# Attention over graph quads: the next quad's scores placed between the products of the first and second unit, one-hots two quads ahead

## The chip, the cores and the metric

The kernel runs on one NeuronCore of a Trainium2 chip. The metric is the device time of one launch in microseconds; less is better. All data starts and ends in HBM; each engine (TensorE = PE, VectorE = DVE, ScalarE = ACT, GpSimd = POOL, SyncE = SP) runs its own instruction stream and waits for the others by semaphores.

## The reference, cut to what matters

`x` is [3125, 768]; there are 50,000 edges `src -> dst`, sorted by `dst`. A two-layer GCN runs first, then one graph attention layer (12 heads of 64), which is the part that the change touches:

```
x = x + GCN(relu(layernorm(x)), edges)            # not touched
h = relu(layernorm(x))
ft = h @ W_fc.T per head;  a1 = <ft, attn_l>;  a2 = <ft, attn_r>
e = leaky_relu(a1[src] + a2[dst], 0.2)
alpha = segment softmax of e over dst             # max, exp, sum, divide
agg = segment_sum(alpha * ft[src], dst)
out = x + relu(h @ W_res.T per head + agg)
```

## The kernel before, in words

The 3125 target nodes are 25 tiles of 128, and a tile is four units of 32 nodes. The edges into a tile are handled in quads. A quad gives each unit four chunks of 128 edges of its own (16 columns of 128 edges) and one shared chunk (column QX = 16). In this data a tile has one quad, so there are 25 quads, and `nth < 1` always holds. The last tile has 53 nodes, so two units (`LU`).

For each quad, GpSimd issues 17 indirect DMAs (`fetch`, line L1089). Each gathers 128 rows of `table3` (12 heads x 65 numbers and the 12 source terms, 792 floats) into `ring`, which has room for two quads. So the gathers of quad q+2 need the room of quad q: `fetch` waits on `used[s]` before the four gathers of unit s, and on `used[US]` before that of the shared chunk. TensorE raises `used[s]` when the products of that unit are done.

What is done for a quad q:

- `next_hot` (VectorE, L1360) makes the one-hot matrix edge -> target; `turn_hot` (PE L1267, ACT L1177) transposes it; `cast_hot` (ACT L1191) makes it float32 for the products.
- `take_terms` (VectorE, L1366 and L1367) copies the source terms out of the ring. It first waits in `rows_landed` for all 17 gathers of its quad.
- `scores` (PE, L1278 to L1285) adds the target terms and the source terms in `ps_s`; only L1285 needs the terms.
- `sloped` (ACT, L1183) multiplies by 0.2; VectorE takes the maximum (L1415), two scans (L1418, L1421: the segment maximum forward and back) and subtracts (L1423).
- PE transposes (L1295), ACT takes the exponential (L1205, `weight`).
- The rows are scaled by the weights in place: units 0 to 2 and the shared chunk by VectorE (L1438 three times, L1443), unit 3 by ACT (L1216, 48 instructions).
- `unit(s)` (PE, L1313, 16 matmuls) multiplies the one-hots into the accumulators; L1324 does the shared chunk.
- The tile before is finished in between: `divide` (VectorE, L1372 to L1376), `natural` (PE, L1236 and L1242), `finish` (VectorE, L1382), then a store.

The order of each engine is written out by hand; there is no scheduler. SyncE loads the slots (indices, two quads ahead), the masks of the scans, and moves the tiles.

## Time and profile before

| | us |
|---|---|
| median of 3 runs | 2235.81 |
| lowest and highest | 2234.13, 2235.86 |
| profiled execution, own time | 2237.61 |
| its span | 2235.8 |
| POOL busy in the span | 1314.7 |
| TensorE, mean granted clock | 0.877 |

The span is the time from the first to the last instruction that the profiler saw. The attention stage is the part from about 1400 us on. A row of the timeline gives start, duration, engine, line, operation, output and inputs, count, and in brackets how long the engine was idle before it and what released it.

### The profile page before, as it was taken

What the parts mean: (1) busy time and instruction counts of PE and PEld (TensorE: products, weight loads), DVE (VectorE), ACT (ScalarE), POOL (GpSimd) and SP (SyncE); (2) the same over time, 40 slices, a digit from 0 to 9 for tenths busy, and PEclk for the clock granted to TensorE, in tenths of its full rate; (3) what the DMA queues carried; (4) which work ended last, traced back from release to release, by engine and by line L of the source; (5) the groups of instructions that cost most, each with busy time, mean ns of one, the idle gap of its engine ahead of it and who ended that gap; (6) DMA issues with size and microseconds to landing.
All of it is one profiled execution on the core that took longest, in us unless ns stands there. A gap on an engine that the chain in (4) does not pass through costs nothing. (4 is left out here: it accounts for less than half of the span.)

```text
span 2235.8 us, 50371 instructions
## 1 busy us (share of the span) xinstructions
PE 1464.5 (66%) x17861; PEld 979.8 (44%) x17862; DVE 839.6 (38%) x1256; ACT 529.1 (24%) x1690; POOL 1314.7 (59%) x1294
## 2 busy tenths in 40 slices
PE   3242787887888578888788867265556555555564
PEld 3141555555555345555555556143334334433442
DVE  9840111111111112222222234365566556655662
ACT  0300011010110000000000026244554455435543
POOL 2014777777776477777777600787665665666530
PEclk9998999999999779999999989578887787878877
DMA  5219999999998599999999826778666766677640
GB/s 186 114 69 281 342 328 331 335 328 333 334 329 296 183 337 329 329 330 326 334 334 329 293 80 271 253 263 291 239 233 224 278 241 222 241 267 256 211 169 33
DMA packets 140710, 587.00 MB, mean 263 GB/s; under 512 B 31465, under 2 KB 33217, under 8 KB 140539
## 3 DMA queue, kind: packets, MB, share of 16 engines
q0 software_dynamic: 100272, 497.49, 63.5%
q1 hardware_dynamic: 33285, 69.50, 8.6%
q10 hardware_dynamic: 7110, 19.43, 2.4%
q8 instruction: 27, 0.44, 0.1%
q14 instruction: 16, 0.13, 0.0%
HBM read 534.62 MB, written 51.71 MB: 262 GB/s over the span
## 5 line engine op out<-in xcount | busy, mean ns | idle before, releaser
L570 POOL DMA_INDIRECT ring_c<-table,slot_c x834 | 794.8, 953 | 323.3 <-issue 300.5
L1089 POOL DMA_INDIRECT ring<-table,slot x417 | 497.5, 1193 | 256.3 <-PE ps_acc L1313 134.6
L1313 PE MATMUL ps_acc<-ring,hot_f 128*32 128x195 f32 x3136 | 183.9, 385 | 183.2 <-ACT ring L1216 117.7
L1216 ACT ACTIVATE ring<-ring,weight x1200 | 290.4, 336 | 0.6
L602 ACT ACTIVATE slot_c<-units 128x8 int32 (+1 forms) x104 | 21.7, 210 | 1058.8 <-DMA ring_c<-table,slot_c 995.6
L1438 DVE TENSOR_TENSOR ring<-ring,weight 128x3120 f32 x73 | 246.3, 3401 | 0.4 <-ACT weight L1205 0.4
L699 DVE TENSOR_TENSOR hots<-iota,units 128x256 f32<-128x256 bf16 x102 | 43.6, 429 | 477.5 <-PE ps_sum0a L655 155.9
L1313 PEld LDWEIGHTS ps_acc<-ring,hot_f 128*32 128x32 f32 x3136 | 104.1, 125 | 249.4 <-ACT ring L1216 127.3
L687 PE MATMUL ps_yb<-weights,sum_tb 128*128 128x512 f32 (+1 forms) x600 | 202.4, 494 | 2.1 <-DVE nodes L730 2.1
L687 PE MATMUL ps_ya<-weights,sum_ta 128*128 128x512 f32 (+1 forms) x600 | 201.9, 493 | 2.1 <-DVE nodes L726 2.1
L655 PE MATMUL ps_sum0a<-ring_c,hots 128*32 128x192 f32 x2000 | 107.6, 374 | 80.0 <-DMA ring_c<-table,slot_c 73.4
L687 PEld LDWEIGHTS ps_yb<-weights,sum_tb 128*128 128x128 f32 x600 | 112.9, 192 | 90.2 <-issue 83.8
L687 PEld LDWEIGHTS ps_ya<-weights,sum_ta 128*128 128x128 f32 x600 | 112.6, 191 | 89.9 <-issue 83.4
L655 PE MATMUL ps_sum0b<-ring_c,hots 128*32 128x192 f32 x2000 | 107.9, 375 | 61.0 <-DMA ring_c<-table,slot_c 54.2
L655 PE MATMUL ps_sum1b<-ring_c,hots 128*32 128x192 f32 x1920 | 100.2, 368 | 48.5 <-DMA ring_c<-table,slot_c 41.1
L1415 DVE TENSOR_TENSOR score<-ps_s,top_g 48x640 f32<-48x640 f32 x25 | 20.5, 818 | 277.9 <-ACT top_g L1183 277.9
L655 PEld LDWEIGHTS ps_sum0a<-ring_c,hots 128*32 128x32 f32 x2000 | 75.4, 124 | 111.9 <-issue 75.9
L655 PE MATMUL ps_sum1a<-ring_c,hots 128*32 128x192 f32 x1920 | 93.5, 348 | 45.6 <-DMA ring_c<-table,slot_c 37.6
L1295 PE MATMUL ps_s<-ident,score 48*128 48x48 f32 x125 | 18.4, 305 | 152.1 <-DVE score L1423 152.1
L655 PEld LDWEIGHTS ps_sum0b<-ring_c,hots 128*32 128x32 f32 x2000 | 75.1, 125 | 93.1 <-issue 62.7
L655 PEld LDWEIGHTS ps_sum1b<-ring_c,hots 128*32 128x32 f32 x1920 | 72.0, 123 | 76.5 <-issue 55.0
L655 PEld LDWEIGHTS ps_sum1a<-ring_c,hots 128*32 128x32 f32 x1920 | 66.8, 116 | 71.8 <-issue 53.8
(238 smaller groups left out, 1680.9 us busy)
## 6 DMA issues: line engine op xcount, KB each, us to landing
ring_c<-table,slot_c POOLq DMA_INDIRECT x834, 5.4
table<-ft SPq DMA_DIRECT2D x25, 396.0 KB, 2.7
table<-nodes SPq DMA_DIRECT2D x25, 384.0 KB, 3.3
table<-nodes ACTq DMA_DIRECT2D x25, 384.0 KB, 5.2
turned_table<-h_t SPq DMA_DIRECT2D x25, 384.0 KB, 2.3
turned_g<-turned_table SPq DMA_DIRECT2D x25, 384.0 KB, 5.9
nodes<-in_x ACTq DMA_DIRECT2D x24, 384.0 KB
out_x<-nodes SPq DMA_DIRECT2D x24, 384.0 KB
```

The costliest lines, as they stand in the source:

```text
L570: eng.indirect_dma_start(out=ring[:, t * QH + k, :], out_offset=None, in_=table, in_offset=bass.IndirectOffsetOnAxis(ap=slot[t][:, k:k + 1 ...
L602: eng.activation(slot[t][:, :], units[:, ds(q, 1), t * QH:(t + 1) * QH + t].rearrange("p a c -> p (a c)"), ACT.Copy).then_inc(slot_ready[t ...
L655: last = eng.matmul(block_of(par, s, g), hot, rows[:, g * GB:(g + 1) * GB], start=start, stop=True, skip_group_check=True)
L687: last = eng.matmul(ps_y[:, c0:c0 + n], sum_t[:, k, :], w[:, k, c0:c0 + n], start=(k == 0), stop=(k == KB - 1))
L699: eng.tensor_tensor(hots[k][:, :, :].rearrange("p (s c) d -> p s c d", c=CPU), iota0[:, :].unsqueeze(1).unsqueeze(2).to_broadcast([P, 2, C ...
L1089: eng.indirect_dma_start(out=ring[:, b * RB + at * FROW:b * RB + (at + 1) * FROW], out_offset=None, in_=table3, in_offset=bass.IndirectOff ...
L1216: last = eng.activation(head, head, ACT.Copy, scale=weight[:, c, mine * H + h:mine * H + h + 1])
L1295: last = eng.transpose(ps_e[:, c, :], score[:, 1 + c * P:1 + (c + 1) * P], ident[0:UH, 0:UH])
L1313: last = eng.matmul(acc_of(s, g), hot_f[:, c, s * UD:(s + 1) * UD], ring[:, x0 + g * GW:x0 + (g + 1) * GW], start=False, stop=True, skip_g ...
L1415: eng.tensor_tensor(score[:, 1:1 + WIN], window(0, WIN), top[:, 1:1 + WIN], ALU.max).then_inc(z_made, 1)
L1438: eng.tensor_tensor(mine, mine, weight[:, 0:CPU, s * H:(s + 1) * H].unsqueeze(3).to_broadcast([P, CPU, H, FH]), ALU.mult).then_inc(scaled[ ...
```

## The change

The change reorders four engines inside a quad and moves two steps across quads.

- VectorE: `take_terms(q + 1)` stood at the end of quad q and now stands after the scaling of unit 0. `next_hot(q + 1)`, which stood before the scalings, becomes `next_hot(q + 2)` at the end of the quad.
- TensorE: `turn_hot(q + 1)` moves ahead of `natural`, and `scores(q + 1)` from behind all products to between unit 0 and unit 1.
- ScalarE: `sloped(q + 1)` is done in the middle of the scaling of unit 3 in quad q, not at the start of quad q+1.
- GpSimd: the gather of the shared chunk is asked for ahead of those of the last unit.

```diff
--- before.py
+++ after.py
@@ -1025,6 +1025,10 @@
             def units_of(j):
                 return LU if isinstance(j, int) and j == NT - 1 else US
 
+
+            def early_of(j):
+                return min(1, units_of(j) - 1)
+
             def node(j):
                 return nodes[:, ds(j, 1), :].rearrange("p a d -> p (a d)")
 
@@ -1089,14 +1093,11 @@
                                 eng.indirect_dma_start(out=ring[:, b * RB + at * FROW:b * RB + (at + 1) * FROW], out_offset=None, in_=table3,
                                                        in_offset=bass.IndirectOffsetOnAxis(ap=slot[:, b, at:at + 1], axis=0)).then_inc(landed[b][s], 16)
                             eng.wait_ge(slot_in, q * 16 + 16)
-                            for s in range(nu):
+                            for s in list(range(nu - 1)) + [US, nu - 1]:
                                 eng.wait_ge(used[s], q + 1)
                                 eng.sem_inc(passed, 1)
-                                for c in range(CPU):
-                                    ask(s * CPU + c, s)
-                            eng.wait_ge(used[US], q + 1)
-                            eng.sem_inc(passed, 1)
-                            ask(QX, US)
+                                for at in (QX,) if s == US else range(s * CPU, (s + 1) * CPU):
+                                    ask(at, s)
                         by_parity(eng, eng.snap(q % 2), gather)
                     last_q, total = quad_bounds(eng)
                     with eng.Fori(0, last_q) as q:
@@ -1194,7 +1195,6 @@
                         mine = units_of(j) - 1
 
                         def follow(q, nth, left):
-                            sloped(q)
                             cast_hot(q, j)
                             with eng.If(nth < 1):
                                 eng.sem_inc(r_exp, 1)
@@ -1214,10 +1214,13 @@
                                 for h in range(H):
                                     head = rows[:, c * FROW + h * FH:c * FROW + (h + 1) * FH]
                                     last = eng.activation(head, head, ACT.Copy, scale=weight[:, c, mine * H + h:mine * H + h + 1])
+                                if c == CPU - 3:
+                                    sloped(q + 1)
                             last.then_inc(scaled[mine], 1)
                         tile_quads(eng, j, follow)
                     turn_hot(0)
                     a2_of(0)
+                    sloped(0)
                     tiles(eng, step)
 
                 @block.tensor
@@ -1294,6 +1297,7 @@
                             for c in range(UC):
                                 last = eng.transpose(ps_e[:, c, :], score[:, 1 + c * P:1 + (c + 1) * P], ident[0:UH, 0:UH])
                             last.then_inc(t_made, 1)
+                            by_parity(eng, eng.snap(q % 2), lambda b: turn_hot(q + 1, 1 - b))
                             with eng.If(nth < 1):
                                 eng.sem_inc(r_hot, 1)
                                 eng.sem_inc(r_all, 1)
@@ -1304,19 +1308,22 @@
                             with eng.Else():
                                 rescale(q, j)
 
-                            def products(b):
-                                def unit(s):
-                                    eng.wait_ge(scaled[s], q + 1)
-                                    for c in range(CPU):
-                                        x0 = b * RB + (s * CPU + c) * FROW
-                                        for g in range(US):
-                                            last = eng.matmul(acc_of(s, g), hot_f[:, c, s * UD:(s + 1) * UD], ring[:, x0 + g * GW:x0 + (g + 1) * GW],
-                                                              start=False, stop=True, skip_group_check=True)
-                                    return last.then_inc(used[s], 1)
-                                turn_hot(q + 1, 1 - b)
-                                eng.wait_ge(hot_cast, q + 1)
-                                for s in range(nu - 1):
-                                    unit(s)
+                            def unit(b, s):
+                                eng.wait_ge(scaled[s], q + 1)
+                                for c in range(CPU):
+                                    x0 = b * RB + (s * CPU + c) * FROW
+                                    for g in range(US):
+                                        last = eng.matmul(acc_of(s, g), hot_f[:, c, s * UD:(s + 1) * UD], ring[:, x0 + g * GW:x0 + (g + 1) * GW],
+                                                          start=False, stop=True, skip_group_check=True)
+                                last.then_inc(used[s], 1)
+
+                            def first_products(b):
+                                for s in range(early_of(j)):
+                                    unit(b, s)
+
+                            def other_products(b):
+                                for s in range(early_of(j), nu - 1):
+                                    unit(b, s)
                                 eng.wait_ge(scaled[US], q + 1)
                                 x0 = b * RB + QX * FROW
                                 for s in range(nu):
@@ -1324,9 +1331,12 @@
                                         last = eng.matmul(acc_of(s, g), hot_f[:, CPU, s * UD:(s + 1) * UD], ring[:, x0 + g * GW:x0 + (g + 1) * GW],
                                                           start=False, stop=True, skip_group_check=True)
                                 last.then_inc(used[US], 1)
-                                unit(nu - 1)
-                            by_parity(eng, eng.snap(q % 2), products)
+                                unit(b, nu - 1)
+                            eng.wait_ge(hot_cast, q + 1)
+                            eng.sem_inc(passed, 1)
+                            by_parity(eng, eng.snap(q % 2), first_products)
                             scores(q + 1)
+                            by_parity(eng, eng.snap(q % 2), other_products)
                         tile_quads(eng, j, visit)
                     turn_hot(0, 0)
                     scores(0)
@@ -1429,7 +1439,6 @@
                                     divide(j - 1, q)
                             with eng.Else():
                                 rescale(q, nu)
-                            next_hot(q + 1)
                             eng.wait_ge(w_made, q + 1)
                             par = eng.snap(q % 2)
                             rows = ring[:, ds(eng.snap(par * RB), RB)].rearrange("p (c f) -> p c f", f=FROW)[:, :, 0:H * FH].rearrange("p c (h x) -> p c h x", x=FH)
@@ -1438,18 +1447,23 @@
                                 eng.tensor_tensor(mine, mine, weight[:, 0:CPU, s * H:(s + 1) * H].unsqueeze(3).to_broadcast([P, CPU, H, FH]), ALU.mult).then_inc(scaled[s], 1)
                                 if s == 0:
                                     eng.tensor_reduce(weight_x[:, :], weight[:, CPU, :].rearrange("p (s h) -> p h s", h=H), mybir.AxisListType.X, ALU.add).then_inc(wx_made, 1)
+                                if s == early_of(j) - 1:
+                                    take_terms(q + 1)
                             eng.wait_ge(wx_made, q + 1)
                             shared = rows[:, QX, :, :]
                             eng.tensor_tensor(shared, shared, weight_x[:, :].unsqueeze(2).to_broadcast([P, H, FH]), ALU.mult).then_inc(scaled[US], 1)
                             if has_before(j):
                                 with eng.If(nth < 1):
                                     finish(j - 1)
-                            take_terms(q + 1)
+                            eng.wait_ge(hot_cast, q + 1)
+                            next_hot(q + 2)
                         return tile_quads(eng, j, visit)
                     bounds = quad_bounds(eng)
-                    next_hot(0)
+                    for b in range(2):
+                        next_hot(b)
                     take_terms(0)
                     tiles(eng, step)
+                    eng.sem_inc(c_chain, 2)
                     divide(NT - 1, bounds[1])
                     finish(NT - 1)
 
```

In TensorE's stream for one quad (tiles 1 to 23, even quads), before; L1278 and L1285 are the scores of the next quad, L1313 the products of the units:

```order
L1295 MATMUL ps_s<-ident,score 128x48 x5
L1236 MATMUL ps_n<-wres_b,turned_g 128x128 x6
L1242 MATMUL ps_n<-o_g,ident 32x192 x16
L1267 MATMUL ps_s<-ident_b,hot 128x128 x5
L1313 MATMUL ps_acc<-ring,hot_f 32x195 x48
L1324 MATMUL ps_acc<-ring,hot_f 32x195 x16
L1313 MATMUL ps_acc<-ring,hot_f 32x195 x16
L1278 MATMUL ps_s<-hot_t,a_blk 48x128
L1285 MATMUL ps_s<-ident,terms 48x128 x5
```

And TensorE's stream at the same place in the changed kernel, where L1270 is the old L1267, L1281 the old L1278, L1316 the old L1313 and L1331 the old L1324:

```order
L1298 MATMUL ps_s<-ident,score 128x48 x5
L1270 MATMUL ps_s<-ident_b,hot 128x128 x5
L1239 MATMUL ps_n<-wres_b,turned_g 128x128 x6
L1245 MATMUL ps_n<-o_g,ident 32x192 x16
L1316 MATMUL ps_acc<-ring,hot_f 32x195 x16
L1281 MATMUL ps_s<-hot_t,a_blk 48x128
L1288 MATMUL ps_s<-ident,terms 48x128 x5
L1316 MATMUL ps_acc<-ring,hot_f 32x195 x32
L1331 MATMUL ps_acc<-ring,hot_f 32x195 x16
L1316 MATMUL ps_acc<-ring,hot_f 32x195 x16
```

The scores of the next quad (L1281 to L1288) have moved ahead of 48 + 16 of the 80 products, and the transposes of the one-hots (L1270) ahead of L1239 and L1245.

In VectorE's stream for one quad, before; L1438 are the scalings, L1366 and L1367 the terms of the next quad:

```order
L1360 TENSOR_TENSOR hot<-iota,slot 128x640
L1438 TENSOR_TENSOR ring<-ring,weight 128x4x780
L1440 TENSOR_REDUCE weight_x<-weight 128x12
L1438 TENSOR_TENSOR ring<-ring,weight 128x4x780
L1438 TENSOR_TENSOR ring<-ring,weight 128x4x780
L1443 TENSOR_TENSOR ring<-ring,weight_x 128x780
L1382 SCALAR_TENSOR_TENSOR nodes<-ps_n,nodes 128x768
L1366 COPY terms<-ring 128x4x4x12
L1367 COPY terms<-ring 128x48
```

And VectorE's stream in the changed kernel, where L1376 and L1377 are the old L1366 and L1367, L1447 the old L1438, L1454 the old L1443, L1392 the old L1382 and L1370 the old L1360:

```order
L1447 TENSOR_TENSOR ring<-ring,weight 128x4x780
L1449 TENSOR_REDUCE weight_x<-weight 128x12
L1376 COPY terms<-ring 128x4x4x12
L1377 COPY terms<-ring 128x48
L1447 TENSOR_TENSOR ring<-ring,weight 128x4x780
L1447 TENSOR_TENSOR ring<-ring,weight 128x4x780
L1454 TENSOR_TENSOR ring<-ring,weight_x 128x780
L1392 SCALAR_TENSOR_TENSOR nodes<-ps_n,nodes 128x768
L1370 TENSOR_TENSOR hot<-iota,slot 128x640
```

The terms of the next quad, with the wait for its landed rows, now stand ahead of the scalings of units 1 and 2 and of the shared chunk; the one-hots went from the front to the end.

## Rows read from the trace of the kernel before

**Rows 1.** Waits, 1700 to 2200 us: who for whom, total, times, longest.

```profile
DVE score L1415 <- ACT top_g L1183: 199.3, 16, 13.1
POOL ring L1089 <- PE ps_acc L1313: 107.1, 20, 9.5
```

**Rows 2.** Timeline of one quad.

```profile
1744.85 0.70 ACT L1183 ACTIVATE top_g<-ps_s 48x640 f32<-48x640 f32 x1 [5.74 <-PE ps_s L1285]
...
1745.58 0.82 DVE L1415 TENSOR_TENSOR score<-ps_s,top_g 48x640 f32<-48x640 f32 x1 [11.69 <-ACT top_g L1183]
...
1746.68 1.49 DVE L1418 TENSOR_TENSOR_SCAN top_g<-same_g,score 48x641 f32<-48x641 bf16 x1 [0.28 <-DVE score L1415]
...
1749.78 0.82 DVE L1423 TENSOR_TENSOR score<-score,top_g 48x640 f32<-48x640 f32 x1
...
1751.53 0.37 ACT L1205 ACTIVATE weight<-ps_s 128x240 f32<-128x240 f32 x1 [5.35 <-PE ps_s L1295]
...
1751.85 0.82 DVE L1360 TENSOR_TENSOR hot<-iota,slot 128x640 bf16 x1
...
1752.58 3.40 DVE L1438 TENSOR_TENSOR ring<-ring,weight 128x3120 f32 x1
...
1756.05 6.71 DVE L1438 TENSOR_TENSOR ring<-ring,weight 128x3120 f32 x2
...
1756.85 1.53 PE L1313 MATMUL ps_acc<-ring,hot_f 128*32 128x195 f32 x32
...
1758.45 11.62 ACT L1216 ACTIVATE ring<-ring,weight  x48
1759.24 1.03 POOL L1089 DMA_INDIRECT ring<-table,slot  x1 [5.75 <-PE ps_acc L1313]
...
1762.68 0.96 DVE L1443 TENSOR_TENSOR ring<-ring,weight_x 128x780 f32 x1
...
1763.56 0.95 DVE L1382 SCALAR_TENSOR_TENSOR nodes<-ps_n,nodes 128x768 f32 x1
...
1770.12 2.83 PE L1313 MATMUL ps_acc<-ring,hot_f 128*32 128x195 f32 x32 [4.45 <-ACT ring L1216]
...
1777.33 0.70 ACT L1183 ACTIVATE top_g<-ps_s 48x640 f32<-48x640 f32 x1 [7.26 <-PE ps_s L1285]
```

**Rows 3.** Timeline of the first quad: gathers beside scalings, the landing, and products.

```profile
1440.91 3.41 DVE L1438 TENSOR_TENSOR ring<-ring,weight 128x3120 f32 x1 [0.39 <-ACT weight L1205]
...
1442.12 3.02 POOL L1089 DMA_INDIRECT ring<-table,slot  x1 [0.30 <-issue]
...
1444.46 2.83 PE L1313 MATMUL ps_acc<-ring,hot_f 128*32 128x195 f32 x32 [2.88 <-DVE ring L1438]
1445.45 3.14 POOL L1089 DMA_INDIRECT ring<-table,slot  x1 [0.31 <-issue]
...
1452.22 0.95 POOL L1089 DMA_INDIRECT ring<-table,slot  x1 [0.30 <-issue]
...
1458.37 0.26 DVE L1366 COPY terms<-ring 128x192 f32 x1 [6.40 <-DMA ring<-table,slot]
```

**Rows 4.** Timeline: gathers that begin during a scan and a one-hot.

```profile
1747.77 1.15 POOL L1089 DMA_INDIRECT ring<-table,slot  x1 [0.30 <-issue]
...
1752.06 1.43 POOL L1089 DMA_INDIRECT ring<-table,slot  x1 [0.30 <-issue]
```

**Rows 5.** Gathers (L1089) from 1480 to 2200 us: issue to landing.

```profile
DMA to landing us min/median/max: 4.4/5.1/5.8
```

**Rows 6.** Windows: busy (instructions) of PE, PEld, DVE, ACT, POOL; PEclk, DMA, GB/s.

```profile
1442.00:1445.00 3.00, 0.54 (x8) 0.46 (x12) 3.00 (x3) 2.94 (x13) 2.88 (x1) 0.50 0.82 279
```

**Rows 7.** Timeline of the last quad.

```profile
2198.14 0.37 ACT L1205 ACTIVATE weight<-ps_s 128x240 f32<-128x240 f32 x1 [5.21 <-PE ps_s L1295]
...
2216.93 2.83 PE L1313 MATMUL ps_acc<-ring,hot_f 128*32 128x195 f32 x32 [11.07 <-ACT ring L1216]
...
2222.43 1.60 PE L1236 MATMUL ps_n<-wres_b,turned_g 128*128 128x128 f32 x12
```

## Prediction

> **What bounds the kernel now.** The page first: POOL is busy for 1314.7 of 2235.8 us (the table above) and no engine is near its span, so the question is which wait ends last. The waits of 1700 to 2200 us (16 quads) show two that matter: DVE waits 199.3 us for `sloped`, 12.5 us a quad, and POOL waits 107.1 us for products to free the ring [rows 1]. The timeline of one quad gives the ring of steps [rows 2]: `sloped` at 1744.85, maximum, two scans, subtraction at 1749.78, weights done at 1751.90, three scalings on DVE to 1762.76; beside them ACT scales unit 3 from 1758.45 to 1770.07, then unit 3's products, then the next quad's scores, and `sloped` again at 1777.33. The reader is to see that scores stand last although nothing in them needs the products. From the weights of this quad (1751.53) to those of the last (2198.14 [rows 7]) are 14 periods of 31.9 us. A quad costs that, 25 times over.
>
> **What the change does to this ring.** It takes the scores, and ACT's wait for unit 3, off the path. On DVE a quad then needs only its own work of [rows 2], so I step through it with the start of the copy of the next quad's terms as 0, durations from [rows 2]:
> - second scaling 0.3 to 3.7 (6.71 for two, so the next starts 3.3 later), third 3.6 to 7.0, shared chunk 6.9 to 7.9, `finish` to 8.8, one-hots 8.7 to 9.5, maximum at 9.4;
> - scans: the first starts 1.10 after the maximum, 10.5 to 12.0, the second to 13.6; subtraction at 13.6; weights done 2.12 after that start (1749.78 to 1751.90), 15.7; first scaling of the next quad from 15.95 to 19.35;
> - then the next copy, if its rows are there: a period of about 20 us. ACT (scalings in two halves of 5.8, `sloped` at about 3.8) has unit 3 ready at 10.3 and is not later. The same count for PE: unit 3's products start by 10.4, its loop has time until 14.7.
>
> So compute alone would go from 31.9 to 20 us. I don't forecast that, because of a wait that the change adds.
>
> **The wait that it adds.** The copy waits for all 17 gathers of quad q+1 (second order difference: it now stands ahead of the scalings of units 1 and 2). Queued behind it on DVE are the scalings of units 1 and 2 of quad q, behind these on PE the products of unit 1, and behind these on POOL the gathers into unit 1's room for quad q+2. POOL can issue only four (unit 0's) before it stands. Before, unit 1's scaling waited for no gather. Priced as a ring:
> - last gather issued to landed: 5.1 (median of 4.4 to 5.8 [rows 5]; 5.89 for the last gather that DVE waited for [rows 3]: 1452.22, copy at 1458.37), plus 0.26 from landing to copy: 5.36;
> - copy and second scaling to 3.7; unit 1's products from 3.75. They take 1.53 at full clock [rows 2] and 2.83 at half. Which? PE will have been idle some 7 us before the scores' last part, as in the first quad, where PEclk was 0.50 through a stretch with 0.54 us of products in 3 us [rows 6] and the first products took 2.83 [rows 3]. I take 2.83: 6.6;
> - products to the first gather 0.86 (1758.38 to 1759.24 [rows 2]): 7.44.
>
> Thirteen gathers are left (four each of units 1, 2, 3, and the shared one). Unhindered, one takes 0.95 and the next follows after 0.30: 12 x 1.25 = 15.0 to the start of the last. Sum without hindrance 7.44 + 15.0 + 5.36 = 27.8.
>
> **The port.** POOL's gathers are hindered by DVE. In the first quad the gathers of 1442.12 and 1445.45 took 3.02 and 3.14: each ended 0.82 after a scaling did (1444.32 + 0.82 = 1445.14) [rows 3]. One begun in a scan took 1.15, in a one-hot 1.43 [rows 4]. Gathers beside the maximum, which reads PSUM, took 0.95. Before, POOL met one or two scalings a quad and stood idle for the others; now its 13 gathers run against nearly all of DVE's work. Stepping, each hindered gather ending 0.82 (0.76 for scans) after the operation:
> 7.44 (shared scaling, ends 8.7), 9.0 (one-hots, 10.3), 10.6 (scan, 12.8), 13.1 (scan, 14.3), 14.6, 15.9, 17.1 (first scaling, 19.35 + 0.82 = 20.2), 20.5, and five more 1.25 apart: the 13th starts at 26.7. Plus 5.36: **32.1 us**. The cover is gone: hindrance costs 4.3.
>
> The Trainium skill ("SBUF — State Buffer", "SBUF: two separate sides") says more: whichever of the two starts first keeps the pair for its whole instruction, so a gather under way would hold DVE up too. By that each of about four operations here would start up to 0.8 us later and the period be some 1 to 2 us longer. The trace disagrees where it can be seen: the gather of 1759.24 lay across the start of a scaling, and the two scalings took 6.71 together [rows 2]. The sum does without it.
>
> **The ends.** Start: in quad 0 the rows of quad 1 come earlier, since DVE no longer scales beside the last gathers (3.02 to 3.14 each [rows 3]): the 15th still starts at 1445.45, the 17th at 1447.95 instead of 1452.22, the copy at 1454.1 instead of 1458.37. Then 22 periods of 32.1 to the copy in quad 22: 2160.3. The last quad has nine gathers, not 17: stepping as above, the last ends its hindrance at 20.2, so the last copy of a loaded quad comes 24.5 later: 2184.8. Weights 15.7 later: 2200.5, against 2198.51 before [rows 7]. After the weights, before: ACT's unit at 18.4, end at 37.3. Now transposing no longer waits for `natural` (about 5 us), but `sloped` in mid-scaling waits for the scores behind unit 0: ACT's unit at 16.6, and the 2.7 us of scores between unit 1's products and `natural` (2219.76 to 2222.43 [rows 7]) are gone: end at 32.9. Sum: 2200.5 + 32.9 = **2233.4** for the profiled span of 2235.8, that is 2.4 less; the profiled execution's own time is 2237.61 and the median 1.8 lower, so 2235.81 - 2.4 = 2233.
>
> Edits that I cost at nothing: one-hots two quads ahead (slots are loaded two ahead, and the wait for `cast_hot` is met since before the weights; 0.8 of DVE if not hidden); the shared chunk asked for before the last unit (POOL follows PE's order; up to one gather, 1.25, if it didn't).
>
> **Rivals.** A measurement of this kernel can tell 0.2%, so no change is 2231.3 to 2240.3.
> - *A. As summed*, 32.1 a period: 2233, own range 2222 to 2245 (landing 4.8 to 5.5, so 0.3 to 0.4 in 22 periods). 0.40.
> - *B. Unit 1's products at full clock.* The scores' last part wakes PE. One gather more fits before the scans: 1.25 less, 30.8, 2233 - 27 = 2206. For it: PE has work just before; in the first quad the second unit took 1.75. Against: the clock in [rows 6]. If it comes with C it is near 2230. 0.28.
> - *C. One gather more is caught (slower).* The first scaling starts at 15.95, and the sixth of the 13 gathers at 15.88, 0.07 earlier. If the scaling is first, that gather takes until 20.1 and all later ones shift by 1.1 to 1.25; the same if it starts late, up to 17.1, since then the seventh is held longer. It decides when the weights are 0.1 us earlier or over 0.6 later, as by unit 3's products at half clock (2.83 [rows 2]). 33.2 a period: 2233 + 24 = 2257. 0.26.
> - *D. Gathers don't bind.* Rows land before DVE wants them and the period falls toward 20 to 28: 22 x 4.3 = 95 less at 27.8, 2138. For it: 17 gathers need 21.3 us. Against: the ring of waits above holds even unhindered. 0.06.
>
> **How the numbers follow.** Faster by over 0.2%: B but its mixed part, 0.24, D 0.06, the lower part of A 0.14: 0.44. Same: A 0.18, B 0.04, C 0.02: 0.24. Slower: C 0.24, A 0.08: 0.32. The likeliest is A. The range leaves out D and the far side of C with a landing of 5.8 (22 x 0.4 more): 2200 to 2262.
>
> **What would show it.** Right: in the changed profile DVE waits about 10 us a quad before the copy of the terms for DMA, POOL waits about 5 us before the gathers of unit 1 for products, gathers of 1.3 to 4.2 us stand beside scans and scalings, and `sloped` is no longer what DVE waits for. PE's products of unit 1 at 2.83 tell A from B; how many gathers start between the second scan and the first scaling tells C. Wrong: a period under 28, rows that land before DVE has done the first scaling, or a wait for unit 3 ahead of the weights.

## The result: the change is 0.3% slower here, and the profile after

| | before | after |
|---|---|---|
| median, us (9 runs each, same chip) | 2235.86 | 2243.34 |
| lowest and highest, us | 2233.99, 2240.58 | 2238.82, 2248.07 |
| profiled execution, own time and span, us | 2237.61, 2235.8 | 2243.34, 2241.6 |
| mean granted clock of TensorE | 0.877 | 0.860 |

The ratio is 1.0032, 95% interval 1.0022 to 1.0042: slower by 0.3%, small but clear of the noise. 2233 with "faster" as the likeliest sign was forecast; the time lies in the range, on the other side of no change.

The waits of the changed kernel, 1700 to 2200 us, answer to [rows 1] (who for whom, total, times, longest):

```profile
DVE terms L1376 <- DMA ring<-table,slot: 205.8, 16, 14.0
ACT top_g L1184 <- DVEq L1421: 202.6, 16, 13.9
PE ps_s L1288 <- DVE terms L1377: 143.3, 16, 10.4
POOL ring L1093 <- PE ps_acc L1316: 97.8, 21, 7.2
```

VectorE no longer waits for `sloped`. In its place it waits 205.8 us for the rows of the next quad to land, before the copy of the terms: 12.9 us a quad, against 12.5 for `sloped` before. One wait was exchanged for another of the same size. POOL waits 6.1 us a quad (97.8 us in 16 quads) for products to free its room. Both are near the signs that the prediction named (about 10 and about 5). The page has the same over the whole span (out<-in, count, then busy and mean ns of one, then idle before):

```profile
L1093 POOL DMA_INDIRECT ring<-table,slot x417 | 504.9, 1211 | 283.0 <-PE ps_acc L1316 153.8
L1376 DVE COPY terms<-ring 128x192 f32 (+1 forms) x26 | 7.1, 272 | 331.3 <-DMA ring<-table,slot 331.3
```

Two successive quads in the timeline of the changed kernel. First one that took 33.0 us from copy to copy:

```profile
1712.03 0.43 DVE L1376 COPY terms<-ring 128x192 f32 x1 [12.83 <-DMA ring<-table,slot]
...
1715.92 2.83 PE L1316 MATMUL ps_acc<-ring,hot_f 128*32 128x195 f32 x32 [0.88 <-DVE ring L1447]
...
1719.59 1.29 POOL L1093 DMA_INDIRECT ring<-table,slot  x1 [7.22 <-PE ps_acc L1316]
...
1722.79 1.99 POOL L1093 DMA_INDIRECT ring<-table,slot  x1 [0.30 <-issue]
...
1725.63 0.82 DVE L1433 TENSOR_TENSOR score<-score,top_g 48x640 f32<-48x640 f32 x1
...
1726.60 0.48 PE L1298 MATMUL ps_s<-ident,score 48*128 48x48 f32 x5 [2.29 <-DVE score L1433]
1726.66 0.94 POOL L1093 DMA_INDIRECT ring<-table,slot  x1 [0.30 <-issue]
...
1727.11 0.37 ACT L1205 ACTIVATE weight<-ps_s 128x240 f32<-128x240 f32 x1 [1.85 <-issue]
...
1727.70 3.41 DVE L1447 TENSOR_TENSOR ring<-ring,weight 128x3120 f32 x1
...
1727.90 4.03 POOL L1093 DMA_INDIRECT ring<-table,slot  x1 [0.30 <-issue]
...
1739.73 0.95 POOL L1093 DMA_INDIRECT ring<-table,slot  x1 [0.30 <-issue]
...
1745.03 0.26 DVE L1376 COPY terms<-ring 128x192 f32 x1 [13.78 <-DMA ring<-table,slot]
...
1758.48 0.82 DVE L1433 TENSOR_TENSOR score<-score,top_g 48x640 f32<-48x640 f32 x1
...
1759.45 0.74 PE L1298 MATMUL ps_s<-ident,score 48*128 48x48 f32 x5 [2.84 <-DVE score L1433]
...
1760.23 0.37 ACT L1205 ACTIVATE weight<-ps_s 128x240 f32<-128x240 f32 x1 [2.67 <-PE ps_s L1298]
...
1760.77 0.94 POOL L1093 DMA_INDIRECT ring<-table,slot  x1 [0.30 <-issue]
1760.82 3.41 DVE L1447 TENSOR_TENSOR ring<-ring,weight 128x3120 f32 x1 [0.18 <-ACT weight L1205]
1762.01 3.03 POOL L1093 DMA_INDIRECT ring<-table,slot  x1 [0.30 <-issue]
...
1771.60 0.95 POOL L1093 DMA_INDIRECT ring<-table,slot  x1 [0.30 <-issue]
...
1777.09 0.26 DVE L1376 COPY terms<-ring 128x192 f32 x1 [12.72 <-DMA ring<-table,slot]
```

The reader is to see the ring: copy at 0, unit 1's products at 3.74 for 2.83 (half clock), first gather into its room at 7.4, and so on up to the 13th gather, the last one of the next quad's rows (1739.73 and 1771.60 here), whose landing releases the next copy (5.3 and 5.5 us after its start). (In the first of the two all is 0.15 later, since its copy took 0.43 and not 0.26.) And the difference between the two quads. In the first the transposes L1298 take 0.48 (granted clock 1.00 in their stretch), the weights come early and the scaling L1447 starts 15.68 after the copy, 0.20 ahead of the sixth gather: that gather takes 4.03 and the quad 33.0. In the other long quads the two start at 15.52 and 15.73. In the second the transposes take 0.74 (granted clock 0.50), the scaling starts 0.05 behind the gather's start; the gather takes 0.94, the next one is held 3.03 instead, and the quad takes 32.1.

Before the change the transposes took 0.74, too, behind a longer idle time of TensorE:

```profile
1750.75 0.74 PE L1295 MATMUL ps_s<-ident,score 48*128 48x48 f32 x5 [6.02 <-DVE score L1423]
```

Where the time went. Of the 22 quads from copy(1) to the copy in quad 22, twelve have the long form (32.4 to 33.3, mean 32.88), nine the short one (31.8 to 32.2, mean 31.98), and the first took 31.36.

| stretch, us | forecast | measured | difference |
|---|---|---|---|
| copy(1) | 1454.1 | 1453.45 | -0.65 |
| 22 periods | 706.2 (32.1) | 713.8 (32.44) | +7.6 |
| copy in quad 22 to last copy | 24.5 | 25.5 | +1.0 |
| to the last weights | 15.7 | 15.3 | -0.4 |
| to the end | 32.9 | 33.6 | +0.7 |

The sum of the differences, 8.2 us, is the distance of the span from the forecast one (2233.4 to 2241.6). Part of the +1.0 has the same cause as the long quads: in quad 23, too, the scaling came first (15.59 against 15.73) and held that gather for 4.09.

### The profile page after: what moved, and what is told of

Read it like the earlier page. It is cut to its first block and busy times, and to the rows that moved or that the text cites. A ratio compares the mean times of both kernels' runs of the same rounds, so it can differ in the third digit from the quotient of the medians.

```text
span 2241.6 us, 50475 instructions
## 1 busy us (share of the span) xinstructions
PE 1472.8 (66%) x17861; PEld 980.9 (44%) x17862; DVE 836.9 (37%) x1257; ACT 532.6 (24%) x1691; POOL 1322.5 (59%) x1294
## 5 line engine op out<-in xcount | busy, mean ns | idle before, releaser
L1093 POOL DMA_INDIRECT ring<-table,slot x417 | 504.9, 1211 | 283.0 <-PE ps_acc L1316 153.8
L1447 DVE TENSOR_TENSOR ring<-ring,weight 128x3120 f32 x73 | 246.8, 3407 | 4.9 <-ACT weight L1205 4.6
L1316 PE MATMUL ps_acc<-ring,hot_f 128*32 128x195 f32 x3136 | 193.5, 400 | 43.2 <-DVE ring L1447 36.2
L1288 PE MATMUL ps_s<-ident,terms 128*48 128x128 f32 x260 | 58.7, 409 | 228.1 <-DVE terms L1377 228.1
L1316 PEld LDWEIGHTS ps_acc<-ring,hot_f 128*32 128x32 f32 x3136 | 107.6, 130 | 117.7 <-DVE ring L1447 62.6
L1288 PEld LDWEIGHTS ps_s<-ident,terms 128*48 128x48 f32 x260 | 46.8, 191 | 253.9 <-issue 251.9
L1376 DVE COPY terms<-ring 128x192 f32 (+1 forms) x26 | 7.1, 272 | 331.3 <-DMA ring<-table,slot 331.3
```

The lines of the kernel that those rows point to most:

```text
L1093: eng.indirect_dma_start(out=ring[:, b * RB + at * FROW:b * RB + (at + 1) * FROW], out_offset=None, in_=table3, in_offset=bass.IndirectOff ...
L1288: last = eng.matmul(window(c * P, P), terms[:, c, :], ident[:, :], start=False, stop=True, skip_group_check=True)
L1316: last = eng.matmul(acc_of(s, g), hot_f[:, c, s * UD:(s + 1) * UD], ring[:, x0 + g * GW:x0 + (g + 1) * GW], start=False, stop=True, skip_g ...
L1447: eng.tensor_tensor(mine, mine, weight[:, 0:CPU, s * H:(s + 1) * H].unsqueeze(3).to_broadcast([P, CPU, H, FH]), ALU.mult).then_inc(scaled[ ...
```

## The experiments

They fell on several chips, and the chips differ far more than the kernels. The kernel before took 2236.64 us on one and 2234.80 on another (called fast chips), and 2838.40 to 2844.35 on four others (slow chips). So every ratio is to the kernel before on the same chip, and kernels from different chips are compared by these ratios. Which chip the change's 2243.34 was taken on is not on record; the kernel before took 2235.86 on it. Where a cell has several runs, the interval is that of the last.

| kernel | fast chip: us, ratio | slow chip: us, ratio |
|---|---|---|
| the change | 2243.34, 1.0032 [1.0022, 1.0042] | 2651.47, 0.9316 [0.9295, 0.9337] |
| terms behind unit 1 | 2179.00, 0.9739 [0.9717, 0.9760] | |
| terms behind unit 2 | 2187.97, 0.9784 [0.9762, 0.9806] | |
| one-hot part alone | 2158.69, 0.9645 [0.9625, 0.9665] | |
| score part alone | | 2648.01, 2650.98, 2650.00; 0.9311, 0.9337, 0.9326 [0.9296, 0.9356] |
| small delay | 2245.58, 1.0034 [1.0021, 1.0047] | |
| larger delay | | 2661.37, 2657.14; 0.9361, 0.9354 [0.9333, 0.9376] |
| delay that reads PSUM | 2229.45, 0.9971 [0.9959, 0.9982] | |
| constant terms | | 2628.41, 2615.47, 2624.92; 0.9255, 0.9220, 0.9236 [0.9200, 0.9272] |
| products to wake TensorE | | 2692.85, 2695.50; 0.9485, 0.9499 [0.9450, 0.9547] |

In the expectations, theory R is the ring of waits that the prediction priced: landing, copy, scaling, products, gathers into the room that these free.

### The place of the wait: terms behind unit 1, or behind unit 2

```diff
             def early_of(j):
-                return min(1, units_of(j) - 1)
+                return min(2, units_of(j) - 1)
```

The copy of the terms, with its wait for the rows, then stands behind the scalings of two units, and the scores behind two units' products. The second kernel has 3.

> The changed kernel, but the terms and the scores of the next quad come after the second unit (copy after the second scaling, scores after the second unit's products), not after the first. Theory R (ring of waits: last gather lands, copy, next scaling, its products, gathers into that unit's room): POOL can now issue eight gathers before it stands, not four, so nine are left behind the wait instead of 13; four gaps of 1.25 go and the ring's unhindered length falls from 27.8 to about 22.8. POOL's own work (17 x 1.25 = 21.3 and 8 to 9 us of hindrance by DVE) then binds: period about 30.2 us against 32.4, total 2185 to 2200. Rival P (POOL is already simply full in the changed kernel, all the loss is hindrance by DVE's operations): DVE does the same operations, period stays 32.0 to 33.0, total 2235 to 2250.

> As terms_after_2, one unit later: copy after all three scalings of VectorE's units, scores after three units' products. Theory R: the wait for landed rows now stands ahead of the shared chunk's scaling alone, five gathers are behind it; ring far below POOL's own work, which binds alone: period about 29.9, total 2180 to 2200, within 10 us of terms_after_2. Rival P: 2235 to 2250. If the compute path counts instead (a later copy gives later scores), it is slower than terms_after_2 by up to 3.3 a quad, 2260.

Measured: 2.6% and 2.2% faster than before, periods of 29.82 and 29.87 us (the mean of 21 periods from weights to weights). The first time lies 6 us under the stated range, the second in it. In the waits of the first of them, 1700 to 2200 us, VectorE's wait for the rows has fallen from 12.9 to 8.2 us each time:

```profile
DVE terms L1376 <- DMA ring<-table,slot: 123.7, 15, 9.0
```

What follows: the loss sits in what is queued behind the new wait. With unit 1's scaling and products ahead of it, the gathers into unit 1's room no longer depend on the landing of this quad's rows. Going on to 3 gave nothing more: the wait for rows fell again (73.0 us in 14), but TensorE's wait for ACT's unit 3 rose from 29.9 us in 17 to 94.4 in 17. The copies, the scores and the products around them moved together; no run moves the wait alone.

### The halves: one-hots two ahead alone, and scores between the products alone

One-hot part alone: one-hots, their early transposes and the order of the gathers are as in the change; terms, scores and slopes stay at their old places.

```diff
-                                if s == early_of(j) - 1:
-                                    take_terms(q + 1)
...
+                            take_terms(q + 1)
```

> The half of the change without its wait: one-hots two quads ahead, their transposes ahead of the residual products, the shared chunk's gather ahead of the last unit's; but the copy of the terms, the scores and their slope stand where they stood before, at the end of a quad and the start of the next. Theory R: the only harm was the wait for landed rows in mid-quad; the earlier transposes let ScalarE start unit 3 about 5 us earlier (1.8 after the weights and not 6.9), which was on the path of the kernel before. The period falls from 31.9 until POOL's own work with hindrance binds, 28 to 29.5, total 2145 to 2185. Rival S (one-hots two ahead or the gather order cost something, or ScalarE's start was hidden by DVE's scalings): 2225 to 2245.

Measured: 2158.69, 3.5% faster than before, inside the stated range; the best kernel of this study, 84.6 us below the change's 2243.34. Its period is 28.89 (quads of 27.5 and 30.0 in turn). Three rows of its timeline:

```profile
1699.83 3.41 DVE L1447 TENSOR_TENSOR ring<-ring,weight 128x3120 f32 x1 [0.19 <-ACT weight L1206]
...
1701.37 11.62 ACT L1217 ACTIVATE ring<-ring,weight  x48
...
1719.82 0.26 DVE L1376 COPY terms<-ring 128x192 f32 x1 [8.06 <-DMA ring<-table,slot]
```

ACT begins unit 3 at 1.54 behind VectorE's first scaling; before it was 5.87 (1752.58 to 1758.45 [rows 2]), since ACT stood at the copy of the transposed one-hots, which TensorE made behind `natural`. That early transposing takes 4.3 us out of the old ring. The period gains only 2.9 to 3.0 of it, because the copy now waits for rows, 5.3 to 8.8 us a quad. All products stand ahead of that wait here. So the useful part of the change was the one I costed at nothing, and with the part that I priced added the gain is gone. That the early transposing brings it is read from these rows; it was not run apart from the one-hots' new place on VectorE and the new order of the gathers.

Score part alone: the one-hots and their transposes as before, the rest as changed. The order of the gathers stayed as in the change, too, although the last of its expectations says otherwise; so neither half tests that order by itself.

```diff
+                                turn_hot(q + 1, 1 - b)
+                                eng.wait_ge(hot_cast, q + 1)
...
-                            next_hot(q + 2)
```

> The other half of the change: the copy of the terms and the scores after the first unit and the slope in mid-scaling, as in the changed kernel, but the one-hots of one quad ahead made before the first scaling and transposed behind the residual products, as before. Theory R: the ring of waits does not contain the one-hots, so the period is that of the changed kernel, 31.5 to 33, total 2225 to 2250; the 77 us that hots_only gained are not lost here, since the ring hides them. If the two halves simply added, this would be 2243 + 77 = 2320.

> The change without its one-hot part: the scores, terms and slopes are moved, the one-hots, their transposes and the order of the gathers are as before. The other half alone took 2159 on a chip on which the kernel before takes 2236, so on such a chip: theory G (the period is the ring of gathers, whatever VectorE's one-hots do) gives about the time of the whole change or more: the one-hot (0.82 us) then lies ahead of the first scaling, which comes to 16.4 or later after the copy, so the seventh gather is held longer, period 32.5 to 33.5, total 2240 to 2265. Rival (the halves add): the one-hot part is worth about 76 us by itself and the score part then costs some 80, so this would be 2300 or more. On a chip on which before takes 2840: 2645 to 2655, as seen twice.

All three runs fell on slow chips: 0.931 to 0.934, the same as the whole change there (0.9316). With the scores moved, the one-hot part is worth nothing on these chips. Whether the halves would add there can't be told, since the one-hot part alone wasn't run on a slow chip; nor was the score part alone on a fast one.

### The phase: three delays of the first scaling

Theory G: a quad is long where the first scaling starts ahead of the sixth gather. Then work added ahead of that scaling should make the kernel faster.

Small delay, four small writes ahead of the first scaling:

```diff
+                            for k in range(4):
+                                eng.memset(idle[:, k * 32:(k + 1) * 32], 0.0)
```

> The changed kernel with four empty writes of 128x32 floats to a scratch tile on VectorE, after the wait for the weights and ahead of the first scaling: work added, about 0.3 us a quad, 25 times. Theory G (in about half of the quads the first scaling starts 15.5 after the copy, ahead of the sixth of 13 gathers at 15.73, which then takes 4.03; in the others it starts at 15.78 and the gather slips through): with 0.3 more the scaling starts after 15.73 in every quad, all periods are 31.9 to 32.3, the twelve long ones lose about 0.9 each: total 2243 - 11 = 2232 (2228 to 2236). Rival: the alternation comes from elsewhere (DMA landing times, TensorE's clock on unit 1), and added work costs what it is or nothing: 2243 to 2251.

Measured: 2245.58, no better. Where the transposes are fast, the scaling moved only from 15.52 to 15.68, still 0.05 ahead of the gather, and in 14 of 22 quads the sixth gather is held. Write, scaling and gather in its timeline:

```profile
1763.89 0.21 DVE L1445 MEMSET idle<- 128x32 f32 x4
1764.02 3.37 DVE L1450 TENSOR_TENSOR ring<-ring,weight 128x3120 f32 x1
1764.06 4.15 POOL L1094 DMA_INDIRECT ring<-table,slot  x1 [0.30 <-issue]
```

The lead of 0.05 need not be the reason. In three of the nine short quads of the unaltered change the transposes took 0.65 to 0.69, the scaling started level with the sixth gather or up to 0.04 ahead of it, and the gather was free all the same:

```profile
1858.80 3.48 DVE L1447 TENSOR_TENSOR ring<-ring,weight 128x3120 f32 x1
1858.84 0.95 POOL L1093 DMA_INDIRECT ring<-table,slot  x1 [0.31 <-issue]
```

In the twelve long ones the lead is 0.20. So which of two starts within 0.05 us counts can't be read from the trace, and here the write, which begins before the gather, may be what held it. The next run bears on that.

Larger delay, one write of 128x384 at the same place:

```diff
+                            eng.memset(idle[:, :], 0.0)
```

> The run delay moved the first scaling by 0.16 us only (15.52 to 15.68 after the copy), still 0.05 ahead of the sixth gather at 15.73, and the long periods stayed. Here one empty write of 128x384 floats stands in the same place, about 0.4 us. Theory G: the first scaling starts at 15.9 to 16.2 in every quad, behind the sixth gather, which takes 0.95 and not 4.03 or 4.15; all periods 32.0 to 32.4, none at 32.8 to 33.1; total about 2234 to 2240, below delay by 6 to 12 although the kernel does more. Rival: the long periods stay and the total is 2245 or more.

This run and its repeat fell on slow chips; before the repeat a held gather in every quad was put down as what would be seen if a write holds gathers too. In both the scaling did start at 15.93, 0.2 behind the gather, and yet the gather was held:

```profile
2132.26 0.38 DVE L1444 MEMSET idle<- 128x384 f32 x1
2132.36 4.36 POOL L1094 DMA_INDIRECT ring<-table,slot  x1 [0.30 <-issue]
2132.56 3.35 DVE L1449 TENSOR_TENSOR ring<-ring,weight 128x3120 f32 x1
```

The gather began during the write, which reads nothing, and was still under way when the scaling came. The test was void: the delay did itself what it should keep off.

A delay that reads PSUM, 128x390 numbers behind the first operation of `divide`, of a size with the larger write:

```diff
+                        eng.tensor_copy(idle[:, :].rearrange("p (s x) -> p s x", s=2), ps_acc[:, :].rearrange("p (s x) -> p s x", s=US)[:, 0:2, 0:GW])
```

> The change with one VectorE copy of 128x390 from PSUM (about 0.45 us) added at the start of the divide step, behind the maximum and scans and ahead of the first scaling. It reads PSUM, so by the theory it does not hold a gather up. Theory G (the first scaling's start against the sixth gather's, 15.73 us after the copy of the terms, decides a quad's length): the first scaling comes behind the sixth gather in nearly every quad, no sixth gather takes over 2 us, all periods are 31.9 to 32.4 us, and although VectorE does 25 x 0.45 = 11 us more, the total is within 0.4% of the unaltered change or below it: on a chip on which the kernel before takes 2236, 2230 to 2240. Rival (the long quads come from something else, such as a landing that varies): the gathers stay held in half of the quads, or the periods of 33 us stay though no gather is held, and the time goes up by up to 11 us, to 2243 to 2255. On a chip on which the kernel before takes 2840 only the sixth gather's duration and the start of the first scaling are to be read; the time is then 2645 to 2665.

Its timeline:

```profile
1722.16 0.55 DVE L1384 COPY idle<-ps_acc 128x390 f32<-128x390 f32 x1
1722.31 0.48 PE L1299 MATMUL ps_s<-ident,score 48*128 48x48 f32 x5 [2.17 <-DVE score L1435]
1722.37 0.95 POOL L1094 DMA_INDIRECT ring<-table,slot  x1 [0.30 <-issue]
...
1723.62 0.95 POOL L1094 DMA_INDIRECT ring<-table,slot  x1 [0.30 <-issue]
1723.75 3.40 DVE L1449 TENSOR_TENSOR ring<-ring,weight 128x3120 f32 x1
...
1724.87 3.10 POOL L1094 DMA_INDIRECT ring<-table,slot  x1 [0.30 <-issue]
```

Although the transposes run at full clock here (0.48), the scaling starts 0.13 behind the sixth gather (1723.62), which takes 0.95. So it does in all of the quads 2 to 22, with fast transposes or slow: the scaling at 15.86 to 16.06, 0.13 or 0.14 behind the gather, no sixth gather over 0.95, periods of 31.4 to 32.6; the mean of the 22 periods is 31.97 against 32.44. The time is 2229.45, just under the stated range; the ratio 0.9971 lies below the whole of the change's interval (on another chip, each against the kernel before on its own): 25 useless copies make the kernel 0.6% faster. The stated rival, 2243 to 2255, is out. Of the 13.9 us between the two spans 10.4 lie in the 22 periods and 1.5 more between the copy in quad 22 and the last, where the same gather is free here.

### What the wait is worth: constant terms

The source terms come from a tile of zeros, so they are left out of the scores; the copy waits for nothing, and the wait for the rows stands ahead of the first scaling and of ACT's unit 3.

```diff
-                        rows_landed(eng, q, bounds, passed)
...
+                        eng.tensor_copy(terms[:, 0:CPU, :], no_terms[:, 0:CPU, :])
```

> The changed kernel, but the source terms are copied from a tile of zeros, so the copy in mid-quad waits for no landed rows; the wait for a quad's own rows stands ahead of its first scaling on VectorE and ahead of unit 3's on ScalarE instead. It leaves the source terms out of the attention scores; all other work and all gathers are the same. Theory R: the ring through unit 1's room is gone, POOL issues without standing at unit 1's room, its own work with hindrance binds: period 28.5 to 30.5, total 2155 to 2205. Rival P (hindrance by DVE alone made the change slow): DVE's operations are the same in kind and number, 2230 to 2250.

Three runs, all on slow chips: 2615.47 to 2628.41, on the one chip that has both 27 us below the change (2624.92 and 2651.47). Before that run 40 to 90 us were put down for theory R and under 10 for rival P; it is neither. The periods are 32.2, 33.0 and 32.8, and no wait in them is put to a landing; another wait ends last there (its waits, 1900 to 2500 us):

```profile
ACT hot_f L1193 <- remote: 247.7, 17, 16.6
DVE rden L1382 <- remote: 200.2, 17, 13.4
```

`divide` reads TensorE's accumulators and the cast to `hot_f` waits for TensorE's last products, so I take both for waits for TensorE, which is slow on those chips (below); the profile says only "remote". For the change on a fast chip this experiment says nothing.

### Waking TensorE

Thirty products of 128x64 behind the first part of the scores, to bring unit 1's products to full clock:

```diff
+                            for k in range(WARM):
+                                eng.matmul(ps_s[:, 320:384], ident[:, :], ident[:, 0:64], start=False, stop=True, skip_group_check=True)
```

> The changed kernel with 30 products of 128x64 floats (identity by identity, into unused columns of ps_s) on TensorE in each quad, behind the scores' first part, where it otherwise stands idle for 8 to 10 us until the terms are copied. Work added to keep the granted clock up. Theory R with rival B of the prediction: unit 1's products take 1.53 and not 2.83, the gathers into unit 1's room start 1.3 earlier and one more fits: periods 1.25 shorter, 31.7 where the first scaling catches the sixth gather and 30.8 where not; total 2205 to 2230. If unit 1's products are not in the ring: 2240 to 2250.

Both runs fell on slow chips: 2692.85 and 2695.50, 41 and 44 us above the change's 2651.47 on another slow chip. Unit 1's products took 1.53 in 20 and in 14 of 24 quads, but the kernel as a whole lost: periods of 31 to 41, and ACT waits for TensorE's scores (164.4 us in 17, 1900 to 2500 us). Whether rival B can be brought about at a profit on a fast chip is open.

### The chips

> The changed kernel itself, unaltered, beside the kernel before, as the anchor of this chip. If the chip is as the first (before 2236): 2243. If it is as the two on which the last eight runs fell (before 2840): there delay_more and scores_only, whose periods differ from the change's by under 1 us by theory R, gave 2648 to 2661, so the change itself should give 2640 to 2665.

> The kernel before, unaltered, for its trace on this chip. Chips differ: on one it took 2236 us, on three others 2840 to 2844. If this is one of the latter, theory T (TensorE's instructions are fed slowly there, so every step that stands behind TensorE on the ring of the quad is longer): the time is 2840, the period of a quad 40 us or more, and the stretch from unit 3's products through the scores to the slopes, 7.3 us on the first chip, takes over 12 us, while VectorE's and POOL's operations keep their durations. Theory D (slower DMA is the cause): the products keep their 2.83 us or less, and the extra time is in waits for landed rows.

> The kernel before, unaltered, for its trace if this is a chip on which it takes about 2840 us (on one of 2236 us it only repeats the trace of before). On such a chip, theory T: TensorE's instructions are fed slowly, so the stretch from unit 3's products through the scores to the slopes, 7.3 us on the first chip, takes over 12 us and the period is 40 us or more, while VectorE's and POOL's operations keep their durations. Theory D (slower DMA): the products keep their 2.83 us or less, and the extra time is in waits for landed rows.

The first ran on a slow chip (2651.47, within 2640 to 2665), the second on a fast one (2232.65, like the first trace), the third on a slow one (2840.31). Two windows of the kernel before, 900 to 1300 us, in the GCN stage, which the change doesn't touch (columns as in [rows 6]); first the fast chip:

```profile
900.00:1300.00 400.00, 326.02 (x3903) 209.29 (x3900) 95.67 (x169) 22.91 (x55) 285.71 (x299) 0.94 0.89 313
```

and the slow chip:

```profile
900.00:1300.00 400.00, 304.00 (x2721) 168.46 (x2720) 60.53 (x110) 19.35 (x44) 201.16 (x212) 0.83 0.68 224
```

In the same time 30% fewer products are done. In the attention stage the kernel before has periods of 40.98 us there, against 31.9. Its timeline on the slow chip shows where they go, in unit 3's products:

```profile
2301.10 1.05 PE L1313 MATMUL ps_acc<-ring,hot_f 128*32 128x195 f32 x2 [1.87 <-issue]
...
2305.78 0.95 POOL L1089 DMA_INDIRECT ring<-table,slot  x1 [0.30 <-issue]
2305.96 0.48 PE L1313 MATMUL ps_acc<-ring,hot_f 128*32 128x195 f32 x1 [1.63 <-issue]
2307.03 0.95 POOL L1089 DMA_INDIRECT ring<-table,slot  x1 [0.30 <-issue]
...
2308.09 0.48 PE L1313 MATMUL ps_acc<-ring,hot_f 128*32 128x195 f32 x1 [1.65 <-issue]
...
2310.20 2.76 PE L1313 MATMUL ps_acc<-ring,hot_f 128*32 128x195 f32 x26 [1.62 <-issue]
...
2316.45 0.70 ACT L1183 ACTIVATE top_g<-ps_s 48x640 f32<-48x640 f32 x1 [15.40 <-PE ps_s L1285]
```

and the windows of that stretch:

```profile
2301.00:2310.00 9.00, 2.95 (x6) 0.81 (x7) 0.00 (x0) 0.05 (x1) 5.45 (x6) 0.50 1.00 403
2310.00:2313.00 3.00, 2.81 (x27) 1.98 (x27) 0.00 (x0) 0.00 (x0) 0.00 (x0) 0.50 0.24 85
```

TensorE has its rows and waits for nothing that the profile shows ("issue"), yet issues one product every 2.1 us, while the gathers of POOL are under way and the DMA engines are busy for all of the window; when they fall to 0.24, 26 products come in 2.76. But busy DMA engines alone don't do it. On the fast chip unit 3's products stand beside the same load:

```profile
1770.00:1773.00 3.00, 2.88 (x33) 1.51 (x34) 0.00 (x0) 0.06 (x1) 2.25 (x3) 0.50 1.03 425
```

There 33 come in 3 us. The stretch from the start of unit 3's products (2301.10) to `sloped` takes 15.35 us; on the fast chip 7.21 (1770.12 to 1777.33 [rows 2]). These are the figures that theory T named, and D is out for this stage: the products don't keep their 2.83, and in the change on a slow chip the last gather's start is 5.0 to 5.6 ahead of the copy, as on the fast one (4.9 to 5.8). The kernel before has these products and the scores on its ring, and pays 8.1 us more a quad for them. The change takes both off the ring, and there it is worth 7.6 to 8.1 us a quad (from 40.98 between weights to 32.92, or 33.3 without the first quads): the same kernel, 6.8% faster.

Whether the products wait for their own instructions, the cause that theory T gives, is not shown. The Trainium skill ("Runtime: NRT & Kernel Launch", "Instruction fetch mechanics") says that an engine fetches its instructions over a DMA queue of its own, and that a taken branch out of what it holds must fetch first; the products stand in branches by parity. The trace doesn't bear it out: the pages count the same 27 and 16 packets on the two instruction queues on the fast and on the slow chip, fewer than the 85 times in 600 us that TensorE stood at "issue" before products on the slow one. As far as these counts are complete, that speaks against fetching; the cause is open.

## Why the prediction was wrong

- **Bound and mechanism: right.** Scores and ACT's unit left the ring, and the wait for landed rows took their place, as the section on the wait that it adds had it. The stepping of the gathers holds to 0.2 us (7.41, 9.01, 10.60, 12.90, 14.5, 15.73 against 7.44, 9.0, 10.6, 13.1, 14.6, 15.9), unit 1's products take 2.83 in every quad, which excludes B, and landing plus copy is 4.9 to 5.8 against 5.36. Period D never came.
- **The step that failed** is "weights done 2.12 after that start", in the list of VectorE's own work, and with it the first scaling at 15.95 for every quad. The 2.12 holds where the transposes run at half clock (1758.48 to 1760.60). In twelve of 22 quads they ran at full clock, the weights were 0.26 earlier, and the scaling started at 15.52, 0.20 ahead of the sixth gather at 15.73: rival C, with the very trigger that it named, "when the weights are 0.1 us earlier". I had taken the transposes of the quad in [rows 2] (0.74, L1295 above) for all quads. But there TensorE stood idle for 6.02 before them; the change puts work on it (products of the shared chunk and of unit 3) close ahead of them, and the idle time is 2.0 to 2.9. (Where they run at half clock the scaling is at 15.78 and not at 15.95, and the gather at 15.73 and not at 15.88; the forecast distance of 0.07 is 0.05.) Price: twelve times 0.78 over the 32.1 of A, less 1.1 for the nine short quads and 0.7 for the first, is +7.6 us, the size of the loss. The delay that reads PSUM took away the effect of the early weights and got 2229.45. That the time still fell into the range is in part luck: it is a mixture of A and C, of which the one or the other was forecast.
- **C was priced too high and as all or nothing.** 33.2 was forecast, 32.88 measured, since a long quad takes only 0.9 more than a short one (a gather of 4.03 against one of 3.03 that comes one later): the scaling that holds it is early, so the hold ends early, at 19.76 and not at 20.1. And A and C were taken as exclusive, with 2233 and 2257; both occur in one run, in turn, and the time lies between.
- **Edits at nothing: wrong for the one-hots.** In the change their gain is hidden behind the landing. Alone, with the early transposing and the gathers' order, they are worth 78 us (2236.64 to 2158.69), by the trace because of the early transposing, not of the 0.8 us on VectorE.
- **The ends** were off by less than 1.1 us each.

That the transposes' clock decides is read from the trace; why it is full in one quad and half in the next stays open. TensorE's idle time before them is 1.98 to 2.31 us where unit 2's products took 2.4 to 2.7, all these at full clock; but with an idle time of 2.8 both 0.48 and 0.74 occur.

## What to carry to other kernels

When a step with a wait for a transfer is moved ahead of work that frees the room for the next transfer, the transfers come to depend on their own landing: put such a wait behind the work that frees the room, or price the loop that it closes. Where one engine's operations hold up another's, as the scalings here hold the gathers, a step that comes earlier can be the dearer one: if two starts lie within 0.3 us of each other in the forecast, give the time as a mixture of both orders, and look for what moves one of them (here a clock) in every quad. Cut a change into its halves before judging it, and on more than one chip: one half was worth 3.5%, and the whole was +0.3% on one chip and -6.8% on another.

## What was not expected of the hardware

- A faster operation made a quad longer: five transposes in 0.48 instead of 0.74 us, and the quad took 32.9 instead of 32.0.
- A gather on GpSimd is held not only by scalings with two inputs in SBUF but also from a plain write of zeros on (begun 0.10 into a write of 0.38, held 4.36 with a scaling behind the write), while a copy out of PSUM of 0.55 leaves it at 0.95, although a scaling follows there too.
- Chips of one kind differ: the kernel before took 2235 to 2237 us on two and 2838 to 2844 on four, with TensorE at one product every 2.1 us beside a DMA share of 1.00, at which the fast chip issued 33 in 3 us.
